# Channel attention: keys, biases and queries in another order at the entry, and the last tile's own scores packed into fewer steps

## The chip, the cores and the metric

One core of one Trainium2 chip. The time is device microseconds (us) of one launch, which works through four batches one after the other. TensorE does the matrix products and transposes, VectorE (DVE), ScalarE (ACT) and GpSimd (POOL) the elementwise work, SyncE (SP) the loads. The engines meet through semaphores alone.

## What is computed

A chain of eight layers with a layer norm behind each, on x of 4 x 512 x 128 in float32. The change lies at the seventh, `_L3_attn_ref`, and at the norm ahead of it:

```
Q = (x @ Wq + bq).reshape(b, s, 16, 64) / 8
K = (x @ Wk + bk).reshape(b, s, 16, 64)
V = (x @ Wv + bv).reshape(b, s, 16, 64)
scores = einsum('bshq,bshk->bshqk', Q, K)      # mask: k > q is left out
w = softmax(scores, axis=-1)
attn = einsum('bshqk,bshk->bshq', w, V)
out = attn.reshape(b, s, 1024) @ Wo + bo
```

The attention runs between the 64 channels of a head, for each token and head by itself: 64 x 64 scores per token and head, half of them masked.

## The kernel before, in words

Tokens lie on the 128 partitions. A batch has NT = 4 tiles of 128 tokens, and the stage works on one after the other. The scores of a tile are cut by `score_chunks` into NC = 18 chunks of up to 1536 columns: 6 early ones (queries of the second half), 8 rectangular and 4 late ones. One step n of the loops in `channel_pe`, `channel_act`, `channel_pool` and `channel_dve` handles one chunk (n counts on over the tiles, c = n % NC is the step within the tile):

- GpSimd multiplies queries with keys into one of five buffers D3 (L1417; semaphore `prod`);
- VectorE takes the largest possible score of each query off (`subtract`, L1463; `d`). The largest scores come from running maxima and minima of the keys (`scan_keys`, L1436: two scans of 1024 columns, both operands in SBUF), multiplied with the queries in PSUM (`maxima`, L1449 to L1451);
- ScalarE takes the exponential in place (L1386; `e`);
- TensorE sums the chunk over its keys by transposing matmuls into one PSUM address (`sum_chunk`, L1285: `den`); VectorE multiplies with the values (`weigh`, L1477; `w`); TensorE sums that too (`num`).

The first OWN = 8 queries of each head are not cut into chunks. ScalarE does their 8 x 16 = 128 rows itself, each in one instruction whose scale is the query and whose bias is the largest score (`own_scores`, L1376; `own`). They are spread over the steps 1 to 14 of a tile, 9 or 10 in each, behind the step's exponential. `sum_own` (L1294) sums them in four parts of 16 matmuls, parts 0 and 1 in step 15 and 2 and 3 in step 16 (`own_den`); VectorE weighs them in steps 16 and 17 (`own_w`), and TensorE sums the weighed ones in step 17 and in the step behind it (`own_num`). The own scores of the next tile use the same buffer, and so wait for `own_num`.

At the end of a tile `finish` takes the reciprocal of the sums (L1491) and multiplies (L1497), and `project_out` applies Wo.

Every order is written out by hand; there is no planner. Entry of the stage, tile 0: `turn_pe` transposes the sum of the layer ahead into four PSUM banks (L499), `norm_dve`, `norm_pool`, `norm_pe` and `norm_act` norm its four tiles and transpose them back into xT, with idle matmuls of `idle_work` (L429) between. Then `fill_qk` makes the two halves of the keys (j = 0, 1) and of the queries (j = 2, 3), each a matmul with the weights (L1254) and one with a bias row (L1255). ScalarE moves all four to SBUF (L1358) and the keys once more in another layout, by head (L1362; `kh`). The scans wait for `kh`, the products of GpSimd and the maxima for all four moves (`qk_sb`).

## Time and profile before

| | |
|---|---|
| three runs, median (lowest to highest) | 3670.2 us (3670.17 to 3671.58) |
| the profiled execution, its own time | 3670.1 us |
| its span in the trace | 3668.5 us |
| busy: PE, DVE, ACT, POOL | 86%, 64%, 54%, 38% of the span |
| mean granted TensorE clock | 0.96 |

The page of the profile begins with the busy time of each engine, goes on with the span in 40 slices, the DMA queues, the chain of work that ended last, and the costliest groups of instructions. A group is one line of the program on one engine; behind the bar stand its busy time, the mean of one instruction in ns, and the idle time of the engine just before, with what ended most of it. A timeline shows instructions in order of time; alike ones of one line that follow one another are merged, with their count behind the x, and idle time before them stands in brackets with its releaser. Matmuls are float32; a normal one shows as two records, a transposing one as one. The first batch's stage begins at 466.85 us and its last tile at 777.05 us; the other batches repeat it about 904 us apart.

### The profile page before, as it was taken

What the parts mean: (1) busy time and instruction counts of PE and PEld (TensorE: products, weight loads), DVE (VectorE), ACT (ScalarE), POOL (GpSimd) and SP (SyncE); (2) the same over time, 40 slices, a digit from 0 to 9 for tenths busy, and PEclk for the clock granted to TensorE, in tenths of its full rate; (3) what the DMA queues carried; (4) which work ended last, traced back from release to release, by engine and by line L of the source; (5) the groups of instructions that cost most, each with busy time, mean ns of one, the idle gap of its engine ahead of it and who ended that gap; (6) DMA issues with size and microseconds to landing.
All of it is one profiled execution on the core that took longest, in us unless ns stands there. A gap on an engine that the chain in (4) does not pass through costs nothing. (4 is left out here: it accounts for less than half of the span.)

```text
span 3668.5 us, 52722 instructions
## 1 busy us (share of the span) xinstructions
PE 3156.6 (86%) x19700; PEld 2207.3 (60%) x19700; DVE 2364.9 (64%) x4289; ACT 1980.3 (54%) x4488; POOL 1393.8 (38%) x1292
## 2 busy tenths in 40 slices
PE   4998998888799898888979889888897988988887
PEld 2556567776365646777536564677743655477773
DVE  3366379994246638999415653999931575499983
ACT  1546267773254528777226442877732654277763
POOL 0223066670031307766004120866501322177740
PEclk9998999999899998999989989999998999999999
DMA  4000100000200010000210001000011000100001
GB/s 131 1 1 1 49 12 1 1 1 24 69 1 1 1 61 1 1 1 1 61 33 1 1 1 61 1 1 1 1 61 33 1 1 10 52 1 1 1 1 63
DMA packets 69372, 68.51 MB, mean 19 GB/s; under 512 B 6077, under 2 KB 49623, under 8 KB 68970
## 3 DMA queue, kind: packets, MB, share of 16 engines
q1 hardware_dynamic: 60288, 56.15, 4.9%
q10 hardware_dynamic: 8810, 8.79, 0.7%
q8 instruction: 162, 2.65, 0.3%
q14 instruction: 112, 0.92, 0.1%
HBM read 63.88 MB, written 1.05 MB: 18 GB/s over the span
## 5 line engine op out<-in xcount | busy, mean ns | idle before, releaser
L1417 POOL TENSOR_TENSOR arena<-arena 128x1536 f32<-128x1536 f32 (+9 forms) x480 | 1020.0, 2155 | 395.6 <-DVE arena L1477 296.5
L1285 PE MATMUL psum<-ident,arena 128*128 128x128 f32 (+7 forms) x7168 | 870.0, 280 | 218.3 <-ACT arena L1386 218.1
L1285 PEld LDWEIGHTS psum<-ident,arena 128*128 128x128 f32 (+7 forms) x7168 | 795.8, 138 | 322.3 <-ACT arena L1386 278.6
L1376 ACT ACTIVATE arena<-arena 128x64 f32<-128x64 f32 (+7 forms) x2048 | 708.4, 486 | 139.4 <-PE psum L1294 139.4
L1477 DVE TENSOR_TENSOR arena<-arena,psum 128x1536 f32<-128x1536 f32 (+9 forms) x480 | 494.9, 1064 | 86.2 <-ACT arena L1386 78.5
L1463 DVE TENSOR_TENSOR arena<-arena,psum 128x1536 f32<-128x1536 f32 (+9 forms) x480 | 494.2, 1063 | 7.8 <-POOL arena L1417 5.8
L449 POOL TENSOR_SCALAR veps<-mv 128x1 f32<-128x1 f32 x128 | 24.7, 193 | 1192.4 <-DVE mv L444 1185.7
L838 POOL TENSOR_SCALAR arena<-arena 128x512 f32<-128x512 f32 (+3 forms) x512 | 265.0, 535 | 544.9 <-DVE arena L800 544.7
L1386 ACT ACTIVATE arena<-arena 128x1536 f32<-128x1536 f32 (+2 forms) x288 | 406.5, 1417 | 114.9 <-DVE arena L1463 114.9
L758 ACT ACTIVATE arena<-arena 128x512 f32<-128x512 f32 (+3 forms) x512 | 282.1, 553 | 209.8 <-DVE arena L793 209.8
L711 PE MATMUL psum<-ident,arena 128*128 128x128 f32 x1280 | 192.7, 294 | 92.9 <-ACT arena L769 63.5
L1063 PE MATMUL psum<-arena,stream 128*128 128x512 f32 x512 | 265.7, 601 | 5.0 <-DVE arena L1184 5.0
L711 PEld LDWEIGHTS psum<-ident,arena 128*128 128x128 f32 x1280 | 147.2, 148 | 191.7 <-ACT arena L769 103.2
L1080 PE MATMUL psum<-arena,stream 128*128 128x512 f32 x512 | 241.2, 595 | 0.0
L1294 PE MATMUL psum<-ident,arena 128*128 128x128 f32 (+7 forms) x2048 | 234.0, 273 | 0.0
L1180 DVE TENSOR_TENSOR arena<-arena,psum 128x512 f32<-128x512 f32 x128 | 88.1, 688 | 215.3 <-PE psum L1080 215.3
L1294 PEld LDWEIGHTS psum<-ident,arena 128*128 128x128 f32 (+7 forms) x2048 | 223.4, 137 | 1.2
L1112 ACT ACTIVATE arena<-psum 128x512 f32<-128x512 f32 x128 | 76.4, 597 | 266.3 <-PE psum L1080 266.3
L1184 DVE TENSOR_TENSOR arena<-arena 128x512 f32<-128x512 f32 x128 | 88.6, 692 | 172.5 <-ACT arena L1114 172.5
L669 PE MATMUL psum<-arena 64*128 64x256 f32 (+3 forms) x1024 | 189.8, 477 | 9.6 <-DVE arena L793 7.7
L793 DVE CUSTOM_DVE_ANT_0 arena<-psum,cmask 128x384 f32<-128x384 f32 (+3 forms) x256 | 112.0, 488 | 119.9 <-PE psum L669 119.9
L727 PE MATMUL psum<-arena 128*64 128x128 f32 x2560 | 186.4, 288 | 0.4
(212 smaller groups left out, 4234.1 us busy)
## 6 DMA issues: line engine op xcount, KB each, us to landing
stream<-in_L_ffn_W SPq DMA_DIRECT2D x160, 256.0 KB, 3.1
arena<-in_L_ffn_h_w SPq DMA_DIRECT2D x8, 1024.0 KB, 8.4
arena<-in_L_ffn_w_w SPq DMA_DIRECT2D x12, 256.0 KB, 4.7
arena<-in_L_ffn_h_w ACTq DMA_DIRECT2D x2, 1024.0 KB
wa<-in_L_attn_W_attn ACTq DMA_DIRECT2D x1, 1536.0 KB
wq<-in_L_attn_Wq ACTq DMA_DIRECT2D x2, 512.0 KB
wo<-in_L_attn_Wo ACTq DMA_DIRECT2D x2, 512.0 KB
x<-in_L_attn_x SPq DMA_DIRECT2D x4, 256.0 KB, 3.7
```

What stands on the lines that cost most here:

```text
L711: last = nc.tensor.transpose(GX[:, half, c:c + P], two(PRG[b % 4])[:, half, c:c + P], ident[:])
L758: nc.scalar.activation(pr, pr, ACT.Exp, bias=nb[:, u:u + 1], scale=-1.0, accum_out=rsum[:, u:u + 1]).then_inc(s["probs"], 1)
L838: nc.gpsimd.tensor_scalar(pr, pr, rinv[:, u:u + 1], 1.0, ALU.mult, ALU.mult).then_inc(s["scaled"], 1)
L1063: nc.tensor.matmul(psO, slot[:, 2 * HID + m * P:2 * HID + (m + 1) * P], HR[n % 3], start=n == 0, stop=top2 and n == NE * NM - 1).then_inc( ...
L1080: nc.tensor.matmul(up_bank(n, j), slot[:, j * HID + m * P:j * HID + (m + 1) * P], XS[e % 2], start=True, stop=True).then_inc(s["up"], 1)
L1285: last = nc.tensor.matmul(ps[ch.half][0:rows, to:to + P], buf[:, c:c + rows], ident[:], start=first, stop=False, is_transpose=True, skip_g ...
L1294: last = nc.tensor.matmul(ps[0][0:rows, 0:P], EA[:, k * NH * OWN:k * NH * OWN + rows], ident[:], start=False, stop=k == HD - 1, is_transpo ...
L1376: nc.scalar.activation(by_key[:, 0:HD - r, j], keys[:, h, 0:HD - r], ACT.Exp, bias=NB[:, j:j + 1], scale=Q3[tt % 2][:, j:j + 1]).then_inc( ...
L1386: nc.scalar.activation(D3[n % 5][:, 0:cols], D3[n % 5][:, 0:cols], ACT.Exp).then_inc(s["e"], 1)
L1417: last = nc.gpsimd.tensor_tensor(of_piece(D3[n % 5], piece), q, keys_on(K3[tt % 2], k, nk, w), ALU.mult)
L1463: last = nc.vector.tensor_tensor(d, d, queries_on(psM[ch.half], ch, piece), ALU.subtract)
L1477: last = nc.vector.tensor_tensor(of_piece(W3[n % 2], piece), of_piece(D3[n % 5], piece), keys_on(psV, k, nk, w), ALU.mult)
```

## The change

At the entry of the stage:

- the bias rows of both halves of the keys are multiplied before the norm's transposes, in the place of six idle matmuls; the weights' product adds to them;
- the queries of the second half (j = 3), which the early chunks use, are made and moved ahead of the first half (j = 2);
- the second half of the keys is laid out by head by VectorE instead of ScalarE; ScalarE lays out the first half by head before it moves it plainly;
- GpSimd starts on three moves instead of four; the maxima of the first half of the queries stand behind the first two subtractions;
- a one-column exponential ahead of the norm loads ScalarE's table there;
- the norm's four transposes go to two banks, two tiles to a bank, and the statistics wait for both tiles of a bank. The wait in pairs holds for the last norm of a batch too (`turn_dve` serves both).

In the last tile of each batch the 128 own rows stand in steps 1 to 10 (12 or 13 in each), their sums in steps 11 and 12, their weighing in steps 12 and 13, and the weighed sums in steps 13 and 14. In the other tiles they stay. The biases come first in `fill_qk` of all tiles.

```diff
-        def turn_pe(pe, m):
+        def turn_pe(pe, m, to):
...
-                nc.tensor.transpose(psR[i], of_tile(rT, i), ident[:]).then_inc(nrm["sumT"], 1)
+                nc.tensor.transpose(to[i], of_tile(rT, i), ident[:]).then_inc(nrm["sumT"], 1)
...
-            return lambda k: dve.wait_ge(nrm["sumT"], NT * (m - 1) + k + 1)
+            return lambda k: dve.wait_ge(nrm["sumT"], NT * (m - 1) + k // 2 * 2 + 2)
...
+        FIRST = (0, 1, 3, 2)
...
-        OWN_STEPS = range(1, NC - 3)
-        OWN_AT = {c: own[len(own) * j // len(OWN_STEPS):len(own) * (j + 1) // len(OWN_STEPS)] for j, c in enumerate(OWN_STEPS)}
+        def own_at(tt):
+            steps = range(1, NC - 3 if tt < NT - 1 else NC - 7)
+            n = len(steps)
+            return {c: own[len(own) * j // n:len(own) * (j + 1) // n] for j, c in enumerate(steps)}
...
-        OWN_DEN = {NC - 3: (0, 1), NC - 2: (2, 3)}
-        OWN_W = {NC - 2: (0, 1), NC - 1: (2, 3)}
-        OWN_NUM = {NC - 1: (0, 1), 0: (2, 3)}
+        OWN_DEN, OWN_W, OWN_NUM = {}, {}, {}
+        for tt in range(NT):
+            at = tt * NC + (NC - 3 if tt < NT - 1 else NC - 7)
+            for j in range(2):
+                OWN_DEN[at + j], OWN_W[at + 1 + j], OWN_NUM[at + 2 + j] = ((tt, 2 * j), (tt, 2 * j + 1)), ((tt, 2 * j), (tt, 2 * j + 1)), ((tt, 2 * j), (tt, 2 * j + 1))
...
-            nc.tensor.matmul(ps, xT[:, tt * P:(tt + 1) * P], w[:, c], start=True, stop=False)
-            nc.tensor.matmul(ps, ones[row:row + 1, :], bqkv3[row:row + 1, c], start=False, stop=True)\
-                .then_inc(c3["qk"], 1)
+            if tt > 0 or j >= 2:
+                fill_bias(pe, tt, j)
+            w, c = (wk3, wq3)[j // 2], slice(j % 2 * 512, j % 2 * 512 + 512)
+            nc.tensor.matmul(qk_bank(tt, j), of_tile(xT, tt), w[:, c], start=False, stop=True).then_inc(c3["qk"], 1)
...
-            for j in range(4):
-                move_qk(0, j)
+            act.wait_ge(s["qk"], 1)
+            move_by_head(0, 0)
+            move(0, 0)
+            move_qk(0, 3)
+            act.wait_ge(s["kh"], 2)
+            move(0, 1)
+            move_qk(0, 2)
...
                 if c == 0:
-                    pool.wait_ge(s["qk_sb"], 4 * tt + 4)
+                    pool.wait_ge(s["qk_sb"], 4 * tt + (4 if tt > 0 else 3))
...
+            dve.wait_ge(s["qk"], 2)
+            nc.vector.tensor_scalar(by_head(0, 1), qk_bank(0, 1).rearrange("p (c h) -> p c h", h=NH), HD ** -0.5, None, ALU.mult)\
+                .then_inc(s["kh"], 1)
             scan_keys(0)
             maxima(0, 1)
-            maxima(0, 0)
             subtract(0)
             subtract(1)
+            maxima(0, 0)
...
-                    idle_work(4, 5)
-                    turn_pe(pe, 1)
-                    norm_pe(pe, 5, (3, 4), 0, (6, 2, 2, 2, 2))
+                    idle_work(1, 5)
+                    turn_pe(pe, 1, psR5)
+                    for j in range(2):
+                        fill_bias(pe, 0, j)
+                    norm_pe(pe, 5, (3, 7), 1, (0, 2, 2, 2, 2))
...
-                    norm_act(act, 5, (3, 4))
+                    nc.scalar.activation(spare[:], mhalf[:, 0:1], ACT.Exp).then_inc(c3["spare"], 1)
+                    norm_act(act, 5, (3, 7))
```

**How the order moves, VectorE at the entry.** Before, from the maxima of the second half (first row) over those of the first half to the subtraction of chunk 0; `c3_qk_sb` counts the moves of keys and queries, `c3_prod` the products, `c3_chain` is VectorE's own:

```order
L1449 TENSOR_TENSOR arena<-psum,arena 128x512 [waits c3_qk_sb,c3_chain]
L1450 TENSOR_TENSOR psum<-psum,arena 128x512
L1451 TENSOR_TENSOR psum<-psum,arena 128x512 [waits c3_chain]
L1449 TENSOR_TENSOR arena<-psum,arena 128x512 [waits c3_qk_sb,c3_chain]
L1450 TENSOR_TENSOR psum<-psum,arena 128x512
L1451 TENSOR_TENSOR psum<-psum,arena 128x512 [waits c3_chain]
L1455 TENSOR_SCALAR arena<-psum 128x128 [waits c3_chain]
L1463 TENSOR_TENSOR arena<-arena,psum 128x1024 [waits c3_prod]
L1463 TENSOR_TENSOR arena<-arena,psum 128x512
```

Now, from the second scan on (the first, and the copy of the keys by head, L1535, stand right ahead of it):

```order
L1467 SCALAR_TENSOR_TENSOR arena<-first,arena 128x1024
L1480 TENSOR_TENSOR arena<-psum,arena 128x512 [waits c3_qk_sb,c3_chain]
L1481 TENSOR_TENSOR psum<-psum,arena 128x512
L1482 TENSOR_TENSOR psum<-psum,arena 128x512 [waits c3_chain]
L1494 TENSOR_TENSOR arena<-arena,psum 128x1024 [waits c3_prod,c3_chain]
L1494 TENSOR_TENSOR arena<-arena,psum 128x512
L1494 TENSOR_TENSOR arena<-arena,psum 128x960 [waits c3_prod]
L1494 TENSOR_TENSOR arena<-arena,psum 128x576
L1480 TENSOR_TENSOR arena<-psum,arena 128x512 [waits c3_qk_sb]
L1481 TENSOR_TENSOR psum<-psum,arena 128x512
L1482 TENSOR_TENSOR psum<-psum,arena 128x512 [waits c3_chain]
L1486 TENSOR_SCALAR arena<-psum 128x128 [waits c3_chain]
```

The subtractions of chunks 0 and 1 stand between the two maxima; the negation that ScalarE's own rows wait for (last row) is behind them all.

**ScalarE at the entry.** Before:

```order
L1112 ACTIVATE arena<-psum 128x512 [waits m2_hid,m2_up] x30
L470 ACTIVATE xT<-psum 128x128 [waits norm_xps] x4
L1358 ACTIVATE arena<-psum 128x512 [waits c3_qk]
L1362 ACTIVATE arena<-psum 128x32x16
L1358 ACTIVATE arena<-psum 128x512 [waits c3_qk]
L1362 ACTIVATE arena<-psum 128x32x16
L1358 ACTIVATE arena<-psum 128x512 [waits c3_qk] x2
L1386 ACT_TABLE_LOAD [waits c3_d]
L1386 ACTIVATE arena<-arena 128x1536 [waits c3_qk_sb]
L1386 ACTIVATE arena<-arena 128x1536 [waits c3_d]
L1376 ACTIVATE arena<-arena 128x64 [waits c3_neg,c3_kh]
```

Now:

```order
L1115 ACTIVATE arena<-psum 128x512 [waits m2_hid,m2_up] x30
L1628 ACT_TABLE_LOAD
L1628 ACTIVATE spare<-mhalf 128x1
L472 ACTIVATE xT<-psum 128x128 [waits norm_xps] x4
L1385 ACTIVATE arena<-psum 128x32x16 [waits c3_qk]
L1381 ACTIVATE arena<-psum 128x512
L1381 ACTIVATE arena<-psum 128x512 [waits c3_qk]
L1381 ACTIVATE arena<-psum 128x512 [waits c3_kh]
L1381 ACTIVATE arena<-psum 128x512 [waits c3_qk]
L1414 ACTIVATE arena<-arena 128x1536 [waits c3_d,c3_qk_sb]
L1414 ACTIVATE arena<-arena 128x1536 [waits c3_d]
L1399 ACTIVATE arena<-arena 128x64 [waits c3_neg,c3_kh]
```

The table load has gone from behind the moves to ahead of the norm's four copies, one of the two copies by head (128x32x16) is gone, and the first own row still waits for `c3_neg`.

**TensorE in the last tile, steps 11 and 12.** Before, step 11 (first four rows) and the head of step 12:

```order
L1285 MATMUL psum<-ident,arena 128x128 [waits c3_w]
L1285 MATMUL psum<-ident,arena 128x128 x11
L1285 MATMUL psum<-ident,arena 128x128 [waits c3_e]
L1285 MATMUL psum<-ident,arena 128x128 x11
L1285 MATMUL psum<-ident,arena 128x128 [waits c3_w]
L1285 MATMUL psum<-ident,arena 128x128 x11
```

Now the same:

```order
L1305 MATMUL psum<-ident,arena 128x128 [waits c3_e]
L1305 MATMUL psum<-ident,arena 128x128 x11
L1305 MATMUL psum<-ident,arena 128x128 [waits c3_w]
L1305 MATMUL psum<-ident,arena 128x128 x11
L1314 MATMUL psum<-ident,arena 128x128 [waits c3_own]
L1314 MATMUL psum<-ident,arena 128x128 x15
L1314 MATMUL psum<-ident,arena 128x128 [waits c3_own]
L1314 MATMUL psum<-ident,arena 128x128 x15
L1305 MATMUL psum<-ident,arena 128x128 [waits c3_e]
```

The rows of L1314 are `sum_own`; they now stand behind step 11's chunk sums, where before there were chunk sums alone until step 15.

## Rows read from the trace of the kernel before

**Rows 1.** The page, a costliest group, the whole execution

```profile
L1285 PE MATMUL psum<-ident,arena 128*128 128x128 f32 (+7 forms) x7168 | 870.0, 280 | 218.3 <-ACT arena L1386 218.1
```

**Rows 2.** Timeline, first batch, entry of the stage: start, length (us), engine, line

```profile
466.85 0.69 DVE L503 SCALAR_TENSOR_TENSOR rT<-xT,psum 128x512 f32<-128x512 f32 x1 [1.22 <-PE psum L1063]
467.77 0.60 PE L499 MATMUL psum<-ident,rT 128*128 128x128 f32 x4
473.43 1.12 PE L1254 MATMUL psum<-wk,xT 128*128 128x512 f32 x2
475.64 0.60 ACT L1358 ACTIVATE arena<-psum 128x512 f32<-128x512 f32 x1 [2.27 <-PE psum L1255]
477.75 0.60 ACT L1358 ACTIVATE arena<-psum 128x512 f32<-128x512 f32 x1 [0.58 <-PE psum L1255]
479.31 4.48 DVE L1436 TENSOR_TENSOR_SCAN arena<-first,arena 128x1024 f32<-128x1024 f32 x2 [6.62 <-ACT arena L1362]
484.54 38.05 POOL L1417 TENSOR_TENSOR arena<-arena 128x1024 f32<-128x1024 f32 x21 [12.30 <-ACT arena L1358]
484.56 1.04 DVE L1449 TENSOR_TENSOR arena<-psum,arena 128x512 f32<-128x512 f32 x1 [0.78 <-ACT arena L1358]
490.30 3.54 DVE L1463 TENSOR_TENSOR arena<-arena,psum 128x1024 f32<-128x1024 f32 x4
492.18 1.28 ACT L1386 ACT_TABLE_LOAD   x1 [7.72 <-DVE arena L1463]
496.24 3.16 ACT L1376 ACTIVATE arena<-arena 128x64 f32<-128x64 f32 x9
```

**Rows 3.** Timeline, third batch: the same two marks

```profile
2277.44 0.69 DVE L503 SCALAR_TENSOR_TENSOR rT<-xT,psum 128x512 f32<-128x512 f32 x1 [1.22 <-PE psum L1063]
2306.16 3.15 ACT L1376 ACTIVATE arena<-arena 128x64 f32<-128x64 f32 x9
```

**Rows 4.** Groups by shape near 480 and near 736 us: busy us, mean ns

```profile
L1436 DVE TENSOR_TENSOR_SCAN arena<-first,arena 128x1024 f32<-128x1024 f32 x2 | 4.5, 2280 | 6.6 <-ACT arena L1362 6.6
L1417 POOL TENSOR_TENSOR arena<-arena 128x1024 f32<-128x1024 f32 x1 | 2.4, 2360 | 12.3 <-ACT arena L1358 12.3
L1417 POOL TENSOR_TENSOR arena<-arena 128x512 f32<-128x512 f32 x1 | 1.3, 1269 | 0.0
...
L1436 DVE TENSOR_TENSOR_SCAN arena<-first,arena 128x1024 f32<-128x1024 f32 x1 | 4.4, 4381 | 0.0
L1417 POOL TENSOR_TENSOR arena<-arena 128x512 f32<-128x512 f32 x1 | 3.3, 3257 | 0.0
```

**Rows 5.** Timeline, ScalarE in the last tile of the first batch

```profile
777.05 3.16 ACT L1376 ACTIVATE arena<-arena 128x64 f32<-128x64 f32 x9 [11.20 <-PE psum L1294]
780.05 1.47 ACT L1386 ACTIVATE arena<-arena 128x1536 f32<-128x1536 f32 x1
781.42 3.14 ACT L1376 ACTIVATE arena<-arena 128x64 f32<-128x64 f32 x9
...
836.78 3.59 ACT L1386 ACTIVATE arena<-arena 128x1536 f32<-128x1536 f32 x3
```

**Rows 6.** Timeline, TensorE at the end of that tile

```profile
838.31 3.27 PE L1285 MATMUL psum<-ident,arena 128*128 128x128 f32 x28 [1.80 <-ACT arena L1386]
841.42 3.66 PE L1294 MATMUL psum<-ident,arena 128*128 128x128 f32 x32
861.51 0.39 PE L434 MATMUL psum<-ident,xT 128*128 128x128 f32 x2
```

**Rows 7.** Timeline, VectorE at the end of that tile

```profile
854.32 3.35 DVE L1491 RECIPROCAL arena<-psum 128x512 f32<-128x512 f32 x1
861.88 0.69 DVE L1497 TENSOR_TENSOR arena<-arena,psum 128x512 f32<-128x512 f32 x1 [4.20 <-PE psum L1294]
```

**Rows 8.** Windows, third and last tile: busy us by engine, then TensorE's granted clock

```profile
726.00:728.00 2.00, 2.00 (x11) 2.00 (x11) 2.00 (x2) 2.00 (x7) 1.17 (x2) 0.50 0.00 0
...
777.00:830.00 53.00, 40.27 (x334) 35.89 (x333) 50.02 (x48) 52.95 (x125) 42.77 (x21) 1.00 0.00 1
```

More of the change, by code:

```diff
@@ L203, in transformer @@
         psR = [psum[:, j, 0:P] for j in (2, 5, 6, 7)]
+        psR5 = [psum[:, j, c * P:(c + 1) * P] for j in (2, 6) for c in range(2)]
         A0_ROWS = [psum[:, j, 0:P] for j in (0, 1, 6, 7)]
@@ L416, in transformer @@
             "d", "e", "w", "den", "num", "attn", "proj", "qk", "qk_sb", "v", "kh", "prod", "chain", "rows",
-            "own", "own_den", "own_w", "own_num", "q_ps", "neg")}
+            "spare", "own", "own_den", "own_w", "own_num", "q_ps", "neg")}
         def x_ready(eng, stage):
@@ L1238, in qk_bank, with by_head @@
             return psum[:, (4, 5, 3, 2)[j], :] if tt == 0 else scratch
+        def by_head(tt, j):
+            return KH[tt % 2].rearrange("p (h c) -> p c h", h=NH)[:, j * HD // 2:(j + 1) * HD // 2, :]
         def fill_qk(pe, tt, j):
@@ L1251, in fill_qk, with fill_bias @@
                     pe.wait_ge(c3["qk_sb"], 4 * tt + 3)
-            w, row, c = (wk3, wq3)[j // 2], 32 * (1 - j // 2), slice(j % 2 * 512, j % 2 * 512 + 512)
-            ps = qk_bank(tt, j)
-            nc.tensor.matmul(ps, xT[:, tt * P:(tt + 1) * P], w[:, c], start=True, stop=False)
-            nc.tensor.matmul(ps, ones[row:row + 1, :], bqkv3[row:row + 1, c], start=False, stop=True)\
-                .then_inc(c3["qk"], 1)
+            if tt > 0 or j >= 2:
+                fill_bias(pe, tt, j)
+            w, c = (wk3, wq3)[j // 2], slice(j % 2 * 512, j % 2 * 512 + 512)
+            nc.tensor.matmul(qk_bank(tt, j), of_tile(xT, tt), w[:, c], start=False, stop=True).then_inc(c3["qk"], 1)
+        def fill_bias(pe, tt, j):
+            row, c = 32 * (1 - j // 2), slice(j % 2 * 512, j % 2 * 512 + 512)
+            nc.tensor.matmul(qk_bank(tt, j), ones[row:row + 1, :], bqkv3[row:row + 1, c], start=True, stop=False)
         def fill_v(pe, tt, j):
@@ L1300, in channel_pe @@
             x_ready(pe, 6)
-            for j in range(4):
+            for j in FIRST:
                 fill_qk(pe, 0, j)
@@ L1318, in channel_pe @@
                 if n < NALL:
-                    for o in OWN_DEN.get(c, ()):
-                        pe.wait_ge(s["own"], (tt + 1) * len(own))
+                    for of, o in OWN_DEN.get(n, ()):
+                        pe.wait_ge(s["own"], (of + 1) * len(own))
                         sum_own(psD, o).then_inc(s["own_den"], 1)
-                if n >= NC - 1:
-                    of = tt if c == NC - 1 else tt - 1
-                    for o in OWN_NUM.get(c, ()):
-                        pe.wait_ge(s["own_w"], of * PARTS + o + 1)
-                        sum_own(psA, o).then_inc(s["own_num"], 1)
+                for of, o in OWN_NUM.get(n, ()):
+                    pe.wait_ge(s["own_w"], of * PARTS + o + 1)
+                    sum_own(psA, o).then_inc(s["own_num"], 1)
                 if n == NALL:
@@ L1373, in own_scores @@
                         act.wait_ge(s["own_num"], tt * PARTS)
-                for r, h in OWN_AT[c]:
+                for r, h in OWN_AT[tt][c]:
                     j = r * NH + h
@@ L1377, in own_scores @@
                                          scale=Q3[tt % 2][:, j:j + 1]).then_inc(s["own"], 1)
-            for j in range(4):
-                move_qk(0, j)
+            act.wait_ge(s["qk"], 1)
[5 more added lines that the diff above has]
+            move_qk(0, 2)
             act.wait_ge(s["qk_sb"], 4)
@@ L1442, in maxima @@
                 if tt == 0 or half == 1:
-                    dve.wait_ge(s["qk_sb"], 4 * tt + 4)
+                    dve.wait_ge(s["qk_sb"], 4 * tt + (4 if tt > 0 or half == 0 else 2))
                 else:
@@ L1479, in weigh @@
                 last.then_inc(s["w"], 1)
-                for o in OWN_W.get(c, ()):
-                    dve.wait_ge(s["own_den"], tt * PARTS + o + 1)
+                for of, o in OWN_W.get(n, ()):
+                    dve.wait_ge(s["own_den"], of * PARTS + o + 1)
+                    if o >= PARTS // 2:
+                        dve.wait_ge(s["v"], 2 * of + 2)
                     e = of_piece(of_own(o), (0, PART, OWN, 0))
```

27 lines of the change are left out of this document (17 added, 10 removed).

## The prediction

> **What bounds the kernel now.** I read the page first: among its costliest groups TensorE's chunk sums (L1285) take 870 us, and TensorE sat idle for 218 us in front of them, waiting for ScalarE's exponential [rows 1]. So in the channel stage TensorE has the most busy time, but ScalarE sets the pace of the steps that hold own rows. Then I read two stretches, because the change touches the stage's entry and its last tile.
>
> The entry, from the sum's start at 466.85 us in the first batch [rows 2]: the first key product starts at 473.43, and ScalarE's first copy follows the product and its bias 2.21 us later. Two such copies are 2.11 us apart, so one half matmul costs 1.055 us, and a copy starts 0.10 behind its end. The scans start at 479.31 and take 4.48; GpSimd starts at 484.54, when all four moves are done; the two maxima take from 484.56 to 490.30; then two subtractions, the table load of 1.28, two exponentials, and the first own row at 496.24. That row is the mark: behind it ScalarE works nearly without a gap through the own steps of the tile, so what the entry gains counts where this row starts. It starts 29.39 us behind the sum's start in the first batch and 28.72 in the third, where TensorE ran at its high clock through the queries [rows 2, 3].
>
> The last tile [rows 5]: its first own row starts at 777.05, the exponentials of steps 2 and 15 at 780.05 and 836.78, and exponential and nine own rows follow one another without a gap, 4.36 us a step. An exponential takes 1.37 to the next instruction (780.05 to 781.42), so an own row 0.33. From there TensorE is full: from 838.31 to 861.51, where the residual's matmul for the output begins, it has no gap, and the last weighed own sums are its last work of the tile [rows 6]. VectorE's reciprocal at 854.32 lies beside them, and its product at 861.88 follows TensorE's end [rows 7]. So behind step 15 the tile lasts as long as TensorE's sums.
>
> **The change, part by part.**
>
> *Keys, biases, queries.* The key biases leave the path behind xT: two matmuls of 1.055 us go into the norm in place of six idle ones. TensorE may come to the first transpose of x some 0.3 us late there; the norm's four tiles are paced by GpSimd, so I cost that at nothing. The wait in pairs costs one transpose, 0.15 (four in 0.60 [rows 2]). Both key halves are then ready at 473.43 + 0.15 + 2.11 = 475.69. VectorE's copy by head is not in the trace. Below, it can't be shorter than the plain ScalarE copy of the same size, 0.60; above, VectorE's product with an operand as far strided takes 1.04 [rows 2]. I take 1.04, since the copy writes with that stride. The scans start at 475.79 + 1.04 + 0.04 = 476.87, 2.44 earlier.
>
> *GpSimd's start.* The late queries are ready at 475.69 + 2.11 = 477.80; ScalarE moves them from 477.90 and the second key half from 478.4, so GpSimd is released at 479.05. That is inside the scans, which last until 481.35. Before, the two never met at the entry. They do meet in the middle of tiles: near 736 us a scan has a record of 4.38 us instead of 2.28, and a product of 512 columns one of 3.26 instead of 1.27 [rows 4]. Each stood still while the other ran, so I take it that one waits for the whole of the other. Whichever goes first, they add: the first scan ends at 479.15, GpSimd's first piece holds the second scan back by 2.1 (4.38 less 2.28) to 481.3, the scan takes to 483.6, and the second piece, let in then, needs 1.0 more (3.26 less 2.28) and ends chunk 0 at some 484.7. The Trainium skill, "SBUF — State Buffer", section "Who interferes with whom", has this as a rule: VectorE with two inputs in SBUF and GpSimd reading SBUF exclude each other for a whole instruction, while one with its other input in PSUM doesn't. By it the maxima and subtractions don't wait for GpSimd; with it the sum is the forecast's, without it the first rival's.
>
> *Order on VectorE.* Chunk 1's product ends 1.27 + 2.3 = 3.6 later, at 488.3 (estimate from [rows 4]: 960 and 576 columns are as many as 1024 and 512). The maxima of the late queries lie before that, 483.6 to 486.4, and so does the first subtraction, which ends before 488.3. The second subtraction (1.75, half of the four-piece row) and the maxima of the early queries with the negation (3.0, half of 5.74 and a little) end at 493.1, and the first own row starts there: 26.25 behind the sum's start. GpSimd (3.6) and VectorE (two instructions of about 1.8 each) need less than ScalarE's 4.36 per step behind it, so it stays the pace. **Gain: 29.39 - 26.25 = 3.1 in two batches, 28.72 - 26.25 = 2.5 in two, 11.2 in all.** I take batch 2 to be like 1 and 4 like 3. The table load of 1.28 is in that: its new place is hidden, as ScalarE waits for the norm's transposes there, and the first exponential no longer carries the mark. Query move j = 2 and its wait on GpSimd at step 6 are hidden behind the scans. In later tiles the bias first or last is the same work.
>
> *Last norm.* The wait in pairs holds there too: 0.15 x 4 = +0.6.
>
> *Own rows in the last tile.* ScalarE's work to the last own row stays the same but for the exponentials of steps 11 to 14, which now come behind it. So the exponential of step 11 starts at 836.78 - 4 x 1.37 = 831.3, and TensorE gets it at 832.8 (1.53 later, as at step 15). That is where TensorE becomes full now: 5.5 us earlier than before, but with four more steps of chunk sums ahead of it, each of 24 transposes. At 28 transposes in 3.11 us (838.31 to 841.42) one costs 0.111, a step 2.67, four steps 10.7. The own sums, 4 x 32 transposes, are full-price on either side. TensorE's end: 832.8 + 10.7 + 23.2 = 866.7, 5.2 later. One more wait: the sums of `den` end with step 17's, and only 20 transposes stand behind them now (2.2 us), not the own sums. So the reciprocal can start only at 866.7 - 2.2 + 0.1 = 864.6, and its 3.35 is no longer beside them; the product that stood at 861.88 starts at 868.0. **Loss: 6.1 per batch, 24.5 in all.** VectorE (its weighing of the own rows is 9 us of some 26 it has left at step 11) and GpSimd (three products left) are done before they are missed.
>
> **Sum.** 3670.1 - 11.2 + 0.6 + 24.5 = 3684.0 us. The profiled execution's 3670.1 is 0.1 under the median, so I leave it. A measurement of this kernel can tell about 0.2%, 7.3 us, from no change: 3662.9 to 3677.5.
>
> **The rivals.**
>
> *Scans and products run side by side* (0.17, with smaller versions of the loss in it). GpSimd then starts at 479.05 and has chunk 1 at 486.2; the own row starts at 491.0, 24.2 behind the sum. Gain 5.2 + 5.2 + 4.5 + 4.5 = 19.4: 3675.8, no change. Against it stand [rows 4].
>
> *TensorE is at its low clock when the dense stretch begins* (0.15). The new steps are 13 x 0.33 + 1.37 = 5.7 us long with 2.7 of sums in them. In the third tile the granted clock stood at 0.50 (1.2 GHz) from 726 to 728 us [rows 8], behind a wait of TensorE. Those 2 us cost it 1.0 us of work; with what the fall takes on both sides of them I price it at 1.7 per batch: 3690.8. In the steps themselves it costs nothing, since 24 transposes at half speed still end within 5.7. The Trainium skill, "TensorE: Matmul & The Clock Gate", section "HAM oscillation — how this bites in real kernels", says that bursts with waits between start at the low clock again and again. By it this would hit every batch; the last tile before, where TensorE waits for about a third of a step, shows a clock of 1.00 throughout [rows 8].
>
> *Faster: the last tile's steps are not ScalarE's* (0.05). If the exponential of step 11 kept its old time, the own sums would fill TensorE's waits in steps 11 to 14, 4.36 - 2.67 = 1.7 each, 6.8 us per batch, and the tile would end so much earlier: 3670.1 - 11.2 + 0.6 - 27.2 = 3632.3. It decides by that start: up to 831.3 - 6.1 = 825.2 the tail gains, behind it loses. Rows without a gap on ScalarE speak against it [rows 5].
>
> *The entry gives nothing* (0.03), because the first own row is held by a wait that I don't see: 3695.2.
>
> **Numbers.** Forecast 0.60. Its own bounds: the copy between 0.60 and 1.04 moves little, as the scans only meet GpSimd otherwise; transposes and waits 1 us per batch. The range goes from the first rival to the second, 3675 to 3692, and leaves out 0.08 and a little. Slower by over 0.2%: 0.60 + 0.15 + 0.03 = 0.78; within 0.2%: 0.17; faster: 0.05.
>
> **What would show it.** Entry: the first own row 26.2 us behind the sum's start; a scan or GpSimd's first pieces with records of over 3 us; no table load behind the moves. Last tile: own rows in packs of 12 or 13, step 11's exponential 54.2 us behind the tile's first own row, TensorE full from there, the reciprocal directly ahead of the product at the end, and the product 91.0 us behind the tile's first own row instead of 84.8. It is wrong if the records at the entry are short, or if the end follows the own rows' last exponential by less than now.

## The result, and the profile after

| | before | changed |
|---|---|---|
| median | 3670.2 us (4 runs, 3668.9 to 3671.6) | 3692.7 us (4 runs, 3692.1 to 3698.8) |
| changed / before | | 1.0065, 95% interval 1.0048 to 1.0083 |
| profiled execution | 3670.1 us, span 3668.5 | 3692.5 us, span 3690.9 |

The change costs 22.5 us. The forecast was 3684.0 with a range up to 3692.0: the sign was right, the size 8.7 us short, and the result lies 0.7 us outside the range.

On the page of the changed kernel TensorE's chunk sums take 886.4 us, where they took 870.0 [rows 1]. Their number is the same, so their records have become longer; the engine waits some 10 us more ahead of them:

```profile
L1305 PE MATMUL psum<-ident,arena 128*128 128x128 f32 (+7 forms) x7168 | 886.4, 283 | 228.5 <-ACT arena L1414 209.8
```

The entry of the first batch, in the timeline of the changed kernel (start, length in us, engine, line; the sum's start, 466.33, is the zero of the times below):

```profile
466.33 0.69 DVE L505 SCALAR_TENSOR_TENSOR rT<-xT,psum 128x512 f32<-128x512 f32 x1 [1.22 <-PE psum L1066]
467.77 1.98 PE L1276 MATMUL psum<-bqkv,ones 1*128 1x512 f32 x4
473.00 1.98 PE L1272 MATMUL psum<-wk,xT 128*128 128x512 f32 x4
475.02 1.02 DVE L1535 TENSOR_SCALAR arena<-psum 128x512 f32<-128x512 f32 x1 [2.77 <-PE psum L1272]
476.07 4.47 DVE L1467 TENSOR_TENSOR_SCAN arena<-first,arena 128x1024 f32<-128x1024 f32 x2
478.29 19.19 POOL L1448 TENSOR_TENSOR arena<-arena 128x1024 f32<-128x1024 f32 x10 [6.49 <-ACT arena L1381]
487.54 1.82 DVE L1494 TENSOR_TENSOR arena<-arena,psum 128x960 f32<-128x960 f32 x2 [1.68 <-POOL arena L1448]
489.27 1.03 DVE L1480 TENSOR_TENSOR arena<-psum,arena 128x512 f32<-128x512 f32 x1
489.39 1.49 ACT L1414 ACTIVATE arena<-arena 128x1536 f32<-128x1536 f32 x1 [1.95 <-DVE arena L1494]
492.43 3.15 ACT L1399 ACTIVATE arena<-arena 128x64 f32<-128x64 f32 x9 [1.55 <-DVE arena L1486]
```

Up to GpSimd's start the steps came as forecast. VectorE's copy by head takes 1.02 us (1.04 taken), the scans start 9.74 us behind the sum's start, where 10.02 was forecast (476.87 less 466.85), and GpSimd 11.96 us behind it instead of 12.20. The first own row stands 26.10 us behind it instead of 26.25. The groups by shape of the same entry show where GpSimd and the scans met:

```profile
L1467 DVE TENSOR_TENSOR_SCAN arena<-first,arena 128x1024 f32<-128x1024 f32 x2 | 4.5, 2278 | 0.0
L1448 POOL TENSOR_TENSOR arena<-arena 128x1024 f32<-128x1024 f32 x1 | 4.4, 4419 | 6.5 <-ACT arena L1381 6.5
```

A piece of 2.36 us [rows 4] has a record of 4.42, and the scans none that is longer. GpSimd's record begins at 478.29, where the second scan's begins too (478.28), and ends at 482.71. It is 2.06 us longer than such a piece takes alone: GpSimd stood for nearly the whole second scan, which ends at 480.54.

The last tile of the first batch, in the timeline, one engine after the other:

```profile
773.12 4.15 ACT L1399 ACTIVATE arena<-arena 128x64 f32<-128x64 f32 x12 [11.32 <-PE psum L1314]
827.35 4.22 ACT L1414 ACTIVATE arena<-arena 128x1536 f32<-128x1536 f32 x3
...
828.88 2.84 PE L1305 MATMUL psum<-ident,arena 128*128 128x128 f32 x24 [1.12 <-ACT arena L1414]
853.38 9.33 PE L1305 MATMUL psum<-ident,arena 128*128 128x128 f32 x84
862.55 0.39 PE L436 MATMUL psum<-ident,xT 128*128 128x128 f32 x2
...
860.64 3.35 DVE L1524 RECIPROCAL arena<-psum 128x512 f32<-128x512 f32 x1
864.02 0.69 DVE L1530 TENSOR_TENSOR arena<-arena,psum 128x512 f32<-128x512 f32 x1
```

The exponential of step 11 starts 54.23 us behind the tile's first own row (54.2 forecast), TensorE has no gap from 55.76 on, the reciprocal stands directly ahead of the product, and the product 90.90 us behind the first own row (91.0 forecast). So much for the first batch. In the other three the same mark stands at 92.4. There TensorE's granted clock is at its lower level, 1.2 GHz, just as the dense stretch (the one without gaps) begins. In the second batch that is at 1738.50, and these are the windows around it (length, TensorE's busy time, granted clock, share of the DMA, GB/s):

```profile
1734.77:1738.77 4.00, 1.23 (x11) 0.93 0.00 0
1738.77:1740.77 2.00, 2.00 (x11) 0.50 0.00 0
1740.77:1742.77 2.00, 2.00 (x16) 0.79 0.00 0
1742.77:1774.77 32.00, 31.70 (x289) 1.00 0.00 1
```

In the same three batches the clock had fallen once before, in the norm at the entry, 4.6 us behind the sum's start (second batch, sum at 1375.22). The first own row stands there at 26.95 to 26.98 instead of 26.10. The windows of that norm:

```profile
1375.22:1379.22 4.00, 4.00 (x23) 1.00 0.48 131
1379.22:1380.22 1.00, 0.97 (x7) 0.79 0.00 0
1380.22:1383.22 3.00, 3.00 (x12) 0.50 0.00 0
```

Summed over the four batches of the two profiled executions, changed less before, from these marks. The batch's second sum stands behind the eighth layer:

| stretch | us |
|---|---|
| sum's start to the first own row | -9.1 |
| first own row of the stage to that of the last tile | -1.5 |
| first own row of the last tile to the product | +28.7 |
| product to the sum behind the eighth layer | -0.1 |
| from there to the next batch's sum, three times, code unchanged but for the last norm's wait | +5.1 |
| ahead of the first sum; behind the last | -0.5; -0.1 |
| all, as the spans (3690.9 less 3668.5) | +22.4 |

### The profile page after: what moved, and what is told of

It reads as the page before. It is cut to its first block and busy times, and to the rows that moved or that the text cites. A ratio compares the mean times of both kernels' runs of the same rounds, so it can differ in the third digit from the quotient of the medians.

```text
span 3690.9 us, 52666 instructions
## 1 busy us (share of the span) xinstructions
PE 3166.7 (86%) x19652; PEld 2220.1 (60%) x19652; DVE 2367.4 (64%) x4293; ACT 1978.6 (54%) x4488; POOL 1403.3 (38%) x1292
## 5 line engine op out<-in xcount | busy, mean ns | idle before, releaser
L1448 POOL TENSOR_TENSOR arena<-arena 128x1536 f32<-128x1536 f32 (+9 forms) x480 | 1031.4, 2175 | 431.7 <-DVE arena L1508 324.4
L1305 PE MATMUL psum<-ident,arena 128*128 128x128 f32 (+7 forms) x7168 | 886.4, 283 | 228.5 <-ACT arena L1414 209.8
L1305 PEld LDWEIGHTS psum<-ident,arena 128*128 128x128 f32 (+7 forms) x7168 | 813.7, 140 | 329.2 <-ACT arena L1414 254.0
L451 POOL TENSOR_SCALAR veps<-mv 128x1 f32<-128x1 f32 x128 | 24.5, 191 | 1169.3 <-DVE mv L446 1162.5
L1314 PE MATMUL psum<-ident,arena 128*128 128x128 f32 (+7 forms) x2048 | 234.0, 273 | 0.0
L1314 PEld LDWEIGHTS psum<-ident,arena 128*128 128x128 f32 (+7 forms) x2048 | 223.4, 138 | 1.0
```

The costliest lines, as they stand in the source:

```text
L1305: last = nc.tensor.matmul(ps[ch.half][0:rows, to:to + P], buf[:, c:c + rows], ident[:], start=first, stop=False, is_transpose=True, skip_g ...
L1314: last = nc.tensor.matmul(ps[0][0:rows, 0:P], EA[:, k * NH * OWN:k * NH * OWN + rows], ident[:], start=False, stop=k == HD - 1, is_transpo ...
L1448: last = nc.gpsimd.tensor_tensor(of_piece(D3[n % 5], piece), q, keys_on(K3[tt % 2], k, nk, w), ALU.mult)
```

## The experiments

Each gives its time against the kernel before on the same chip; "mark at the entry" is the first own row behind the sum's start, "mark of the last tile" the product behind that tile's first own row. Unless said otherwise the edit is made on the changed kernel.

**The two halves apart.** Entry alone, and the packed own rows alone (on the kernel before):

```diff
-            steps = range(1, NC - 3 if tt < NT - 1 else NC - 7)
+            steps = range(1, NC - 3)
...
-            at = tt * NC + (NC - 3 if tt < NT - 1 else NC - 7)
+            at = tt * NC + NC - 3
```

> The changed kernel with the last tile's own rows spread over steps 1 to 14 again, as before; all of the entry's change stays. If the two parts simply add (the forecast's steps), the last tile's product stands again 84.8 us behind that tile's first own row, the first own row 26.1 to 27.0 us behind the sum's start, and the time is 3659 to 3663 us. If the loss of the changed kernel comes from the entry (a clock that falls elsewhere because of it), the time stays over 3670 us. If packing the own rows was the gain and the entry the loss, it is over 3692 us.

> The kernel before with only the last tile's own rows in steps 1 to 10; the entry as before. By the forecast's terms the last tile grows by 6.1 us per batch without a fall of TensorE's clock there (3694.7 us) and by 7.6 us with one (3700.6 us). If the extra 1.5 us of three batches came from the entry's change alone, it stays at 6.1 in all four. If the tail is not slower by itself, the time stays within 3670 to 3677 us.

Measured: entry alone 3661.1 us (0.9971, 0.9959 to 0.9984), 10.4 less than before; marks at the entry 26.98, 26.11, 26.94, 26.09, those of the last tile 84.8. Packed rows alone 3699.1 us (1.0071, 1.0054 to 1.0088), 27.5 more; mark of the last tile 90.9 in all four batches. So the entry gains and the last tile loses, each about as forecast in size. But 27.5 - 10.4 is 17.1, and together they cost 22.5. The intervals of the two are some 5 and 6 us wide to either side, so the times alone don't show that the halves fail to add. The marks do: packed alone the last tile loses 4 x 6.07 = 24.3 us, and with the entry's change 28.7. Alone, neither shows the 92.4.

The packed rows alone have the same long steps, and the clock falls four times in each of their last tiles as well. But the last fall begins 50.2 us behind the tile's first own row and is over when the dense stretch begins at 55.8. The windows of the second batch, where these are 1741.1 and 1746.74:

```profile
1741.00:1745.00 4.00, 3.89 (x20) 0.57 0.00 0
1747.00:1779.00 32.00, 32.00 (x296) 1.00 0.01 1
```

In the changed kernel's first batch, without a fall in the norm, the last fall begins at 50.3 us too. In the other three it begins at 55.4 and lasts to 58.8, so that some 3.0 us of the dense stretch run at 1.2 GHz. At half speed those cost 1.5 us, which is the 1.48 measured. The time of the packed rows alone is 3.2 us over 4 x 6.07 although the mark is without a fall: in the profiled execution its first sum comes 3.3 us later than before, and the three stretches of unchanged code take 4.3 more.

**How many steps.** Own rows of the last tile up to step 12, and up to step 15 with their sums in steps 16 and 17 and all four weighed sums behind the last chunk:

```diff
-            steps = range(1, NC - 3 if tt < NT - 1 else NC - 7)
+            steps = range(1, NC - 3 if tt < NT - 1 else NC - 2)
...
+                if tt < NT - 1:
+                    OWN_DEN[at + j], OWN_W[at + 1 + j], OWN_NUM[at + 2 + j] = parts, parts, parts
+                else:
+                    OWN_DEN[at + 1 + j], OWN_W[at + 1 + j] = parts, parts
+        OWN_NUM[NALL] = tuple((NT - 1, o) for o in range(PARTS))
```

> The changed kernel with the last tile's own rows in steps 1 to 12 instead of 1 to 10. By the sum, each step that the end of the own rows is moved ahead costs TensorE's 2.67 us less ScalarE's 1.37, so 2.6 us for two steps instead of 5.2 for four, and the reciprocal stays hidden or shows partly: the tile takes 87.4 to 88.4 us from its first own row to the product, 91.0 now; the time is 3673 to 3680 us. If the loss is a wait on the own rows' parts rather than such a trade, it jumps back to 84.8 or stays at 91 to 92.4.

> The changed kernel with the last tile's own rows in steps 1 to 15, one step later than before, their sums in steps 16 and 17, their weighing there too and all four weighed sums behind step 17. If TensorE's remaining sums against ScalarE's remaining exponentials set the tile's end, moving the own rows back by a step gains TensorE's last bound step (3.1 us for its 28 transposes) less 1.37: the product stands 83.1 us behind the tile's first own row, 84.8 in e1, and the time is 6 to 7 us under e1. If the end is set by the chain of sums, weighing and weighed sums of the own rows, it comes out at 86 us or more, and the time over e1.

Measured: to step 12, 3676.6 us (1.001, 1.0001 to 1.002; single executions 3669.6 to 3682.2, the profiled one the slowest), mark 88.34 in one batch and 90.0 in the three whose dense stretch began at the low clock. To step 15, 3645.1 us (0.9935, 0.9918 to 0.9952), mark 83.15 in all four. That is 16.0 us under the entry alone, where 6 to 7 were expected. The tail gives 6.7 of it. In the profiled executions, 11.8 apart, the norm without a fall gives 1.7 more, and most of the rest lies outside the stage. The order is 83.15, 84.8, 88.3, 90.9 for own rows up to step 15, 14, 12 and 10: packing them tighter is the wrong direction, since it puts whole chunks behind them. The timeline of the version to step 15, where the tile's first own row is at 774.14, shows what is left there:

```profile
836.78 3.28 PE L1310 MATMUL psum<-ident,arena 128*128 128x128 f32 x28 [1.04 <-ACT arena L1419]
849.93 7.15 PE L1319 MATMUL psum<-ident,arena 128*128 128x128 f32 x64
...
851.91 3.35 DVE L1529 RECIPROCAL arena<-psum 128x512 f32<-128x512 f32 x1
857.29 0.69 DVE L1535 TENSOR_TENSOR arena<-arena,psum 128x512 f32<-128x512 f32 x1 [2.02 <-PE psum L1319]
```

TensorE becomes full only 62.6 us behind the first own row, and the reciprocal lies beside the weighed sums again.

**Do GpSimd and the scans shut each other out?** Entry alone, with GpSimd held until both scans are done:

```diff
+                if n == 0:
+                    pool.wait_ge(s["chain"], 1)
```

> As e1, and GpSimd's first product waits besides for the end of both scans. If one of the two engines stands still while the other works on two SBUF operands, GpSimd's start during the scans was worth nothing: the first own row stays where e1 has it, within 0.2 us, and the time is that of e1. If they ran side by side, GpSimd loses the 2.2 us that it ran beside the scans: the first own row comes some 2 us later, 8 us in all.

Measured: 3658.4 us (0.996, 0.9946 to 0.9974), marks at the entry 26.38 and 27.22, twice each, 0.28 more than without the wait. The groups by shape of this kernel's entry:

```profile
L1469 DVE TENSOR_TENSOR_SCAN arena<-first,arena 128x1024 f32<-128x1024 f32 x2 | 4.5, 2281 | 0.0
L1450 POOL TENSOR_TENSOR arena<-arena 128x1024 f32<-128x1024 f32 x1 | 2.4, 2361 | 8.8 <-DVE arena L1469 8.8
```

Holding GpSimd back by 2.3 us costs 0.28: it had hardly worked in that time. That settles the rival of side by side, and the direction too: here GpSimd waited for the second scan. The two records begin within 0.01 us of each other in every batch of the entry alone, and each time the scan went first. In the kernel before, at the place of [rows 4], a product came 0.7 us behind the start of the first scan and ahead of the second, and there the second scan was the one that stood:

```profile
732.25 6.58 DVE L1436 TENSOR_TENSOR_SCAN arena<-first,arena 128x1024 f32<-128x1024 f32 x2
732.97 6.93 POOL L1417 TENSOR_TENSOR arena<-arena 128x1024 f32<-128x1024 f32 x2 [1.96 <-PE psum L1285]
```

**The table load and the order of the maxima.** Both on the entry alone: without the exponential that loads the table ahead; and with the early queries' maxima ahead of the subtractions, as before the change:

```diff
-                    nc.scalar.activation(spare[:], mhalf[:, 0:1], ACT.Exp).then_inc(c3["spare"], 1)
```

```diff
             maxima(0, 1)
+            maxima(0, 0)
             subtract(0)
             subtract(1)
-            maxima(0, 0)
```

> As e1, without the one-column exponential ahead of the norm, so that the table loads in front of the first exponential again. By the forecast the load is no longer on the path: the first own row waits for the negation behind the early queries' maxima, so it stays where e1 has it and the time is e1's within 2 us. If the load is on the path, the first own row comes 1.3 us later in each batch, 5 us in all.

> As e1, with the early queries' maxima ahead of the two subtractions again, as before. In the changed kernel's trace VectorE idles 0.70 and 1.68 us for GpSimd's products in front of the two subtractions. If the maxima fill that time, the second subtraction ends at about the same time, 489.3 to 489.8 in the first batch, and the first own row follows the second exponential at 24.9 to 25.1 us behind the sum's start instead of 26.1: 4 to 5 us under e1. If the forecast's reason for the new order holds (the subtractions first free the path), the first own row comes later than in e1.

Measured: without the load ahead 3658.3 us (0.9964, 0.995 to 0.9979), marks 26.12, 26.12, 26.97, 27.28: as with it but for 0.3 us in the last batch, so the early load brings nothing that shows in the time. Maxima first: 3653.8 us (0.9947, 0.993 to 0.9963), marks 25.90, 25.04, 25.87, 25.04. The timeline of this kernel's second batch, with the sum at 1370.72:

```profile
1385.00 1.05 DVE L1480 TENSOR_TENSOR arena<-psum,arena 128x512 f32<-128x512 f32 x1
1387.79 1.06 DVE L1480 TENSOR_TENSOR arena<-psum,arena 128x512 f32<-128x512 f32 x1
1390.59 0.29 DVE L1486 TENSOR_SCALAR arena<-psum 128x128 f32<-128x128 f32 x1
1390.80 3.54 DVE L1494 TENSOR_TENSOR arena<-arena,psum 128x1024 f32<-128x1024 f32 x4
1392.70 1.48 ACT L1414 ACTIVATE arena<-arena 128x1536 f32<-128x1536 f32 x1 [8.46 <-DVE arena L1494]
1394.37 1.48 ACT L1414 ACTIVATE arena<-arena 128x1536 f32<-128x1536 f32 x1 [0.19 <-DVE arena L1494]
1395.76 3.14 ACT L1399 ACTIVATE arena<-arena 128x64 f32<-128x64 f32 x9
```

Both maxima lie behind each other, and the subtractions follow them without the waits of 0.70 and 1.68 us for GpSimd's products that stand in the changed kernel. The change's new order of maxima costs 1.07 us a batch. With the maxima first the second exponential comes 0.6 us later (23.65 us behind the sum's start instead of 23.06), but the negation is done before it, and the own rows follow it at once. In the changed kernel they wait 1.55 us more for the negation. In two of the four batches of that run a later tile was 1.0 us longer (281.7 instead of 280.6 from the first to the last tile's first own row). The median is 7.3 us under the entry alone, where 4 to 5 were expected, with single executions from 3645.3 to 3659.2.

**What the fall of the clock has to do with it.** First the key biases put back beside the key products (on the entry alone), with the six idle matmuls in the norm again:

```diff
-                    for j in range(2):
-                        fill_bias(pe, 0, j)
-                    norm_pe(pe, 5, (3, 7), 1, (0, 2, 2, 2, 2))
+                    norm_pe(pe, 5, (3, 7), 1, (6, 2, 2, 2, 2))
```

> As e1, with the biases of the keys multiplied beside the keys again and the six idle matmuls back in the norm. On the path the scans start 2.1 us later and GpSimd with them; as VectorE idles 1.7 us for GpSimd, and GpSimd for the scans, the first own row comes 2.1 us later, 28.2 us behind the sum's start. If the fall of TensorE's clock in the norm (it costs the first own row 0.85 us where it comes) is a matter of what TensorE does there, it is gone in all four batches and the own row stands at one place; if it is a matter of when the batch comes, some batches still have it. The time is 5 to 9 us over e1.

Measured: 3662.6 us (0.998, 0.997 to 0.999), mark at the entry 28.39 in all four, with no fall of the clock in the norm. By the mark the biases' move is worth 2.3 us a batch, and it is the part behind which the falls in the norm appear. The median doesn't show it: it is 1.5 us over the entry alone, where 5 to 9 were expected, and single executions go from 3657.5 to 3672.0, of which the profiled one is the slowest. Then idle matmuls in the last tile, where TensorE waits for the own rows:

```diff
+                if tt == NT - 1 and EARLY + 2 <= c < NC - 7:
+                    pe.wait_ge(s["rows"], NT - 1)
+                    idle_work(2, 8)
```

> The changed kernel with eight idle matmuls in each of the last tile's steps 8, 9 and 10, where TensorE has 2.7 us of sums in a step of 5.7. Nothing is left out of the computation. Theory A (the 1.5 us between 90.9 and 92.4 in the last tile is TensorE's low clock in the first microseconds of the dense stretch): the granted clock stays at 1.00 from 52 to 64 us behind the tile's first own row, the product stands 90.9 us behind it in all four batches, and the time falls by 3 x 1.5 = 4.5 us to some 3688, give or take what moves in the unchanged layers. Rival B (the 1.5 us is a wait of another engine that only coincides with the low clock): the clock is mended and the product stays at 92.4. Rival C (the clock falls in spite of the idle work): both stay.

Measured: the mark of the last tile is 90.91, 90.91, 90.92 and 90.90. But the time is 3692.95 us (1.0059, 1.0046 to 1.0073), as without the idle work. The windows of this kernel's second batch, whose dense stretch begins at 1744.81:

```profile
1741.05:1757.05 16.00, 15.01 (x137) 1.00 0.00 1
1757.05:1781.05 24.00, 22.59 (x205) 1.00 0.00 1
1781.05:1783.05 2.00, 2.00 (x16) 0.74 0.00 0
1783.05:1785.05 2.00, 1.75 (x9) 0.50 0.00 0
```

Theory A holds for the last tile: with the clock at 1.00 the 1.5 us are gone, 4.4 in all. But in three batches the clock now falls 93 us behind the first own row, in the output's product and the norm that follow, and the stretch from the product to the sum behind the eighth layer is 78.15 us there instead of 77.07: 3.3 back. Ahead of the first sum this execution takes 3.8 us more, and the three stretches of unchanged code take 3.5 less (434.7, 434.7 and 429.9 us, against 434.1, 434.3 and 434.3). The profiled execution is 0.7 us under the changed kernel's.

**The best version.** Own rows to step 15 and maxima first; then the same with three idle matmuls behind each transpose of the norm; then the same as the first with one bias half ahead of the sum's transposes:

```diff
-                    norm_pe(pe, 5, (3, 7), 1, (0, 2, 2, 2, 2))
+                    norm_pe(pe, 5, (3, 7), 1, (0, 3, 3, 3, 3))
```

```diff
-                    idle_work(1, 5)
+                    fill_bias(pe, 0, 0)
                     turn_pe(pe, 1, psR5)
-                    for j in range(2):
-                        fill_bias(pe, 0, j)
+                    fill_bias(pe, 0, 1)
+                    idle_work(1, 3)
```

> The changed kernel with the last tile's own rows in steps 1 to 15 and with the early queries' maxima ahead of the subtractions. Nothing is left out of the computation. Theory: the two gains don't touch each other: first own row 25.04 or 25.90 us behind the sum's start (with and without a fall of the clock in the norm), product 83.15 behind the last tile's first own row, and 3 to 4 us less than the version with own rows to step 15 alone (3645.1): about 3641.5. Rival (what is won at the entry is lost again at the end of the third tile, where one run with the maxima first had tiles 1 us longer): 3645.

> As the combined version, with three idle matmuls in place of two behind each transpose of x in the last norm before the stage. Nothing is left out of the computation. Theory A (the fall of TensorE's clock in that norm comes from its gaps of 0.3 us in steps of 0.9): no fall in the norm, and the first own row 25.0 us behind the sum's start in all four batches. Rival B (the 2 us of bias matmuls, with one row of input each, in place of idle work are what lets the clock fall, in spite of their being back to back): the fall stays in two or three batches, with 25.9 there. Either way the time moves by at most 2 us here, beside what moves in the unchanged layers.

> As the combined version (median 3648.7, single executions from 3643.5 to 3655.9), with the first bias half put ahead of the sum's transposes in place of the five idle matmuls there, and the second behind them with three idle matmuls: the stretch of 2 us in which TensorE has nothing but one-row bias matmuls is cut into two of 1 us. Nothing is left out of the computation. Theory (that stretch is what lets the clock fall in the norm in some batches; no batch of the three kernels without it fell there): no fall in the norm in any batch, first own row 25.0 us behind the sum's start in all four, and single executions closer together, within some 5 us, at about 3643.5. Rival (the falls come from the gaps of the norm or from something further ahead): falls in some batches, and executions spread over 12 us as in the combined version.

Measured: combined 3648.7 us (0.9944, 0.993 to 0.9957; single executions 3643.5 to 3655.9), with marks of 25.04 and 83.15 to 83.17 in all four batches of the profiled one, which is the fastest of the five. The marks add as the theory says; the medians don't show it, as 3648.7 and 3645.1 (own rows to step 15 alone) lie inside each other's spread. With more idle work 3651.4 us (0.9949, 0.9935 to 0.9962): the clock fell in the norm in two batches all the same, and the mark was 26.44 there, not the 25.9 that rival B had. With the biases split 3647.7 us (0.9937, 0.9924 to 0.9951): falls in two batches, and earlier, at 2.7 instead of 4.6 us behind the sum; the marks are 25.63, 25.61, 25.09 and 25.10, and from there to the last tile it takes 1.0 us longer in all four. My theory for that run (the 2 us of one-row matmuls in a row let the clock fall) expected none and is wrong in that form. What stands is a count: with a key bias in the norm the clock fell there in 21 of 44 profiled batches, and in none of 12 without. Which work in that norm it is, and why only in some batches, stays open.

## Why the prediction was right or wrong

- **Keys, biases, queries; GpSimd's start; order on VectorE: right, with some luck.** 26.10 us where 26.25 was forecast, and the copy, the scans' start and GpSimd's release within 0.3 us of the sum. One detail was other than told: the forecast let GpSimd's first piece hold the second scan back, while the second scan went first and GpSimd stood. So the scans end 14.2 us behind the sum's start and not 16.8, and VectorE has idle time ahead of its subtractions that the forecast didn't see; the order of the maxima that uses it is 1.07 us a batch faster. Chunk 1 was ready at nearly the same time either way (21.2 us behind the sum's start, 21.45 forecast), as the two add whichever goes first. The Trainium skill, "SBUF — State Buffer", section "Who interferes with whom", was taken for the lock, and the added wait agrees with it: +0.28 us, where work side by side would have made it some 2.2.
- **The entry's gain, 11.2 us: measured 9.1.** Without a fall of the clock it would be 116.1 less 4 x 26.1 = 11.7. Three batches with the fall in the norm give 2.6 back. The forecast costed the six idle matmuls that the biases replaced at nothing, with "the norm's four tiles are paced by GpSimd". GpSimd does pace them at the high clock. At the low one TensorE does: four idle matmuls there take 1.06 us instead of 0.61, and the next transpose of x waits for them.
- **Last norm, +0.6: not seen.** Behind the sum at the end of the fourth batch, where nothing follows but this norm and the store, the kernel takes 0.1 us less than before.
- **Own rows in the last tile: the mechanism right, 24.5 us forecast, 28.7 measured.** Every sign is there. At the high clock the loss is 6.07 a batch, 24.3 in all. The missing 4.4 are three batches with 1.48 more each, and that is the second rival, priced at 1.7 and given 0.15. The mistake was to treat it as all or nothing and as unlikely: the steps had become 5.6 us long with 2.7 us of sums in them, and the clock of 1.00 in [rows 8] was that of steps of 4.4 us, which says nothing of longer ones. But the long steps alone are not enough either: with the packing alone the clock falls in them and is back before the dense stretch in all four batches. The fall reached the dense stretch in just the batches with a fall in the norm at the entry: in three of four of the changed kernel and in three of four with rows to step 12. So the 4.4 us come from both halves together, and the term put at nothing, the six idle matmuls, has its part in them. That the one fall moves the other is read from which batches have both; no run forces a fall in the norm. The Trainium skill, "TensorE: Matmul & The Clock Gate", section "HAM oscillation — how this bites in real kernels", has bursts with waits start at the low clock time and again; the trace agrees in that the clock fell four times in each last tile of the changed kernel and never in one of the kernel before. That it hits every batch's dense stretch, as the forecast read it, holds in three batches of four, and in none of four with the packing alone.
- **No term for the unchanged code: +5.1 us.** From the sum behind the eighth layer to the next batch's sum, before: 432.3, 434.0, 431.3; after: 434.1, 434.3, 434.3. But for the last norm's wait nothing of the code changed there. The low clock lies at slightly other places in it, and the stretch between the last two norms ahead of the stage, which took 152.9 to 155.5 us, takes 155.6 or 155.7 in the last three batches. With the packing alone, which has no fall in the norm, the three stretches are 434.0 each, 4.3 us over before. That such shifts follow from the falls in the stage is argued, not shown: the runs show only that these stretches take between 429.9 and 434.7 us in all variants, and that the three of a run together lie between 1291.8 (the last run) and 1302.7 (the change). The range had nothing for it. Between the first tile's and the last tile's first own row the kernel takes 1.5 us less than before, for which there was no term either; most of it is one batch that took 281.6 us before and takes 280.6 now.
- **The rivals.** Side by side is refuted by the added wait. The faster case decides by the start of the step 11 exponential, 54.2 us behind the first own row and not under 48.1. The entry that gives nothing is refuted by the entry alone.

So three steps failed, 12.1 us together. The idle matmuls that left the norm were costed at nothing, and the clock fell there: 2.6 us. The low clock in the dense stretch was held apart as a rival where it was a part of the sum: 4.4 us. A kernel's unchanged stretches were taken as fixed: 5.1 us, whose cause stays open. Against them stand the 0.6 of the last norm that is not seen, the 1.5 between the tiles, 0.6 by which the entry without a fall did better than forecast, and 0.9 of smaller ones, which leaves the 8.5 us between 3684.0 and the profiled execution's 3692.5.

## What to carry to other kernels

Ask of work that is packed into fewer steps what then stands behind it: four chunks of sums went behind the last own row, out of the shade of ScalarE, and spreading the rows over one step more than before won 1.7 us a batch where packing lost 6.1. Where TensorE fills only half of its steps, price the low clock into the sum, and ask where its falls will lie: the same packed steps lost nothing to it with the old entry and 1.5 us in three batches of four with the new one. And read a local gain in the whole kernel's time: idle work kept the clock up in the last tile, and it fell 38 us later instead. A single profiled execution can be the fastest or the slowest of a kernel whose executions lie up to 14 us apart, so its marks say more of a change than its time.

## What was not expected of the hardware

- GpSimd's product and the second of two scans that follow each other came within 0.01 us of each other, and the product stood (record 4.42 us instead of 2.36) in every batch, though in the kernel before a scan could also be the one that stood (4.38 [rows 4]).
- The granted clock fell to 0.50 in the norm behind 4.00 us in which TensorE's records leave no gap (second batch), idle, transposing and one-row bias matmuls among them, in some batches of the same program and not in others.
- The places of the clock's falls go together across 300 us: in the batches with a fall in the norm those of the last tile come 5.1 us later in the changed kernel (the last of them at 55.4 instead of 50.3 us behind its first own row), and so into the dense stretch, which begins at 55.8. With rows to step 12 it is 4.6 us, with idle work in the tail 4.8.
